# A graph attention layer on one core: wider VectorE instructions in the attention block, and the carried product ahead of the weighted ones

## The chip, the cores and the metric

The kernel runs on one core of one Trainium2 chip. The metric is the device time of one execution in microseconds (us), as the median of several runs. On-chip memory has 128 partitions; a shape like 128x1024 means 128 partitions by 1024 elements of each.

## The reference

The program computes four graph layers, one after the other, on 6250 nodes with 16 features and 206250 edges sorted by their target node: a graph convolution, an edge-conditioned convolution, a sheaf layer and an attention layer. Each is applied to a normalised copy of the features and its result added to them. The change touches the last, the attention layer:

```python
w_m = (efeat @ W_msg + b_msg).reshape(E, in_f, -1)
w_a = (efeat @ W_attn + b_attn).reshape(E, in_f, -1)
h_src = feat[src][:, :, None]
e1 = w_m * h_src
e2 = w_a * h_src
seg_max = jax.ops.segment_max(e2, dst, num_segments=N)
ex = jnp.exp(e2 - seg_max[dst])
denom = jax.ops.segment_sum(ex, dst, num_segments=N)
attn = ex / denom[dst]
ft = jax.ops.segment_sum(e1 * attn, dst, num_segments=N)
return ft.sum(axis=1)
```

`e1` and `e2` have 16 x 16 = 256 elements for each edge.

## The kernel before

**Tiling.** The edges lie in quads: four edges with the same target. Each of the 128 partitions has 440 quads, and the stage "attn" (L2435 to L2815) takes them in 110 blocks of `QB` = 4. For a block, `T` holds two planes (`t` = 0: attention value `e2`; `t` = 1: message `e1`) of 4 quads x 4 edges x 256 elements; `X` holds `exp` of the first plane and its product with the second. `T` has two buffers, chosen by the block's parity, and `X` has one. `walk` (with `At`, which turns a block's number into semaphore values) writes the first and last blocks out and runs the others in a loop of two blocks a turn.

**The engines, each with its own hand-written order:**

- GpSimd (L2513) gathers the source nodes' features (`got`) and the edge lines, 16 + 2 indirect transfers a block. SyncE loads lines and stores the maxima (`tops`) and sums (`sums`) of each block.
- TensorE (L2549): `matrices(at, q)` (L2569) computes for the four edges of quad `q` both 256-element rows into `pw`, in PSUM, once `times` has freed it. `quad_sum(at, q)` adds up the four edges of a quad by four matmuls with the identity (L2578), which wait on `s_prod`, and adds the running sum of the quads before by a fifth (L2585): for quad 0 that is `carried`, for the others the sum that ScalarE has just copied. The order in a block is: `quad_sum` of quads 1, 2, 3 of the block before, each followed by `matrices` of the next block's same quad; then three of four matmuls of `quad_sum(at, 0)`, `matrices(at+2, 0)` in between, and the rest of `quad_sum(at, 0)`.
- ScalarE (L2608): `weights` (L2639) is the exponential of one quad, once all subtractions of the block are done; `scales` computes the factor for the running sum; `put_state` (L2658) copies a quad's running sum from PSUM, which the next `quad_sum` waits for; `tops_out` (L2644) copies the maxima.
- VectorE (L2696), function `a_block`. In order, where `times(nxt, q)` (L2715) multiplies the next block's matrices by the gathered features, two instructions a quad: first half of `times(nxt, 0)`; `larger` over pairs of edges into `two` (L2730), one instruction for two quads; second half of `times(nxt, 0)`; `larger` over what is left (L2730); `forward(0)` (L2737), the running maximum; first half of `times(nxt, 1)`; `forward(1)`; second half; `forward(2)`, `forward(3)`; three `back` (L2743), which carry the maximum back to the first quad, with the subtractions `below` (L2748) of quads 3, 2 and 1 in between; `drop` (L2791) and `below(0)`; `times(nxt, 2)`; `product(0)` (L2755); the running sum times its factor into `carried` (L2799, which waits on ScalarE's factor and last state copy); `product(1)`; `times(nxt, 3)`; `product(2)`, `product(3)`.

`ch.do` counts an instruction on a semaphore of VectorE's own, and `ch.wait(n)` waits until instruction `n` has written its result. `turn_wait` is a wait on a semaphore followed by an increment of another.

## Time and profile before

| what | value |
|---|---|
| time, median of 3 runs | 8973.12 us (8966.02 to 8974.08) |
| span of the profiled execution | 8951.1 us (its own time is not given; the median lies 22.0 us above this span) |
| instructions | 135582 |
| busy share of the span | VectorE 84%, TensorE 81%, GpSimd 71%, ScalarE 54% |
| attention blocks | from about 5805 to 8845 us of the span |

The profile comes from one execution. The engines are called PE (TensorE; PEld is its weight load), DVE (VectorE), ACT (ScalarE), POOL (GpSimd) and SP (SyncE) in it.
### The profile page before, as it was taken

To read this page: it belongs to the slowest core of one execution; us is meant where nothing else is said; L and a number is where in the kernel's file an instruction comes from. 1 tells how busy PE (TensorE), PEld (TensorE's weight loads), DVE (VectorE), ACT (ScalarE), POOL (GpSimd) and SP (SyncE) were. 2 spreads that over 40 slices of the span, in tenths; PEclk is the share of its full clock that TensorE was granted. 3 is DMA by queue.
4 is the path that set the end of the run, shared out by engine and by line. 5 is a ranking of instruction groups with operands and counts; after the bars stand their busy time and mean duration, and the time that the engine had idled before them with its cause. 6 is when DMAs were issued, how large, how long until landed. Compare 5 with 4: busy or idle time off the path is not lost. (4 is left out here: it accounts for less than half of the span.)

```text
span 8951.1 us, 135582 instructions
## 1 busy us (share of the span) xinstructions
PE 7229.0 (81%) x35152; PEld 4078.3 (46%) x35152; DVE 7510.0 (84%) x11807; ACT 4799.3 (54%) x7730; POOL 6388.3 (71%) x6335
## 2 busy tenths in 40 slices
PE   3888857888888088888888889488888888888884
PEld 3776744555555055555555555233333333333331
DVE  7999956777777388888888888499999999999997
ACT  5999956666666056556666656233333333333333
POOL 6777767777776577777777777376777777677674
PEclk9899967888887589999999999789999999999997
DMA  4222221121111111111111111122222222222223
GB/s 154 65 64 61 64 40 44 45 45 46 46 45 38 20 28 28 33 28 33 28 31 29 29 32 17 20 65 82 75 75 76 75 82 76 75 76 75 81 77 99
DMA packets 499695, 493.19 MB, mean 55 GB/s; under 512 B 181075, under 2 KB 396906, under 8 KB 498731
## 3 DMA queue, kind: packets, MB, share of 16 engines
q1 hardware_dynamic: 299595, 371.60, 12.5%
q0 software_dynamic: 199904, 119.78, 9.7%
q14 instruction: 171, 1.40, 0.1%
q8 instruction: 25, 0.41, 0.0%
HBM read 240.96 MB, written 249.95 MB: 55 GB/s over the span
## 5 line engine op out<-in xcount | busy, mean ns | idle before, releaser
L2525 POOL DMA_INDIRECT attn_got<-tab,attn_line x1760 | 1925.6, 1094 | 778.7 <-issue 504.4
L1983 POOL DMA_INDIRECT sheaf_got<-tab,sheaf_idx x1612 | 1692.1, 1050 | 489.9 <-issue 474.8
L2578 PE MATMUL attn_q<-attn_X,ident 128*128 128x512 f32 x3520 | 1716.2, 626 | 101.1 <-ACT attn_S L2658 92.5
L2072 PE MATMUL sheaf_acc<-sheaf_hot_hi,sheaf_wide 128*128 128x392 bf16 x6696 | 1350.5, 344 | 282.7 <-DVE sheaf_hot_hi L2275 280.9
L1508 POOL DMA_INDIRECT nnconv_got<-tab,nnconv_idx x1116 | 1081.9, 969 | 400.0 <-issue 320.9
L2578 PEld LDWEIGHTS attn_q<-attn_X,ident 128*128 128x128 f32 x3520 | 651.4, 198 | 1190.6 <-issue 1190.6
L2715 DVE TENSOR_TENSOR attn_T<-attn_w,attn_got 128x1024 f32<-128x1024 f32 x880 | 1054.5, 1220 | 150.4 <-PE attn_w L2569 115.2
L2658 ACT COPY attn_S<-attn_q 128x512 f32<-128x512 f32 x440 | 255.9, 582 | 1530.4 <-PE attn_q L2585 1530.4
L1173 POOL DMA_INDIRECT gcn_got<-tab,gcn_idx x868 | 825.9, 952 | 302.3 <-issue 274.7
L2072 PEld LDWEIGHTS sheaf_acc<-sheaf_hot_hi,sheaf_wide 128*128 128x128 bf16 x6696 | 653.6, 106 | 819.1 <-issue 489.7
L1267 PE MATMUL gcn_acc<-gcn_hot,pieces 128*128 128x512 f32 x2604 | 740.2, 442 | 193.9 <-ACT gcn_hot L1321 126.6
L2569 PE MATMUL attn_w<-src_hi 32*128 32x512 f32 x3520 | 567.1, 715 | 274.7 <-DVE attn_T L2715 273.7
L1197 DVE SCALAR_TENSOR_TENSOR gcn_hot<-gcn_key,key_of,gcn_one 128x512 fp32r<-128x512 f16 x1116 | 750.4, 743 | 4.2 <-DMA gcn_blk<-src_blk 4.2
L1740 DVE TENSOR_TENSOR nnconv_prod<-nnconv_w,nnconv_got 128x1024 f32<-128x1024 f32 x434 | 490.6, 1143 | 268.0 <-PE nnconv_w L1543 267.4
L1267 PEld LDWEIGHTS gcn_acc<-gcn_hot,pieces 128*128 128x128 f32 x2604 | 541.1, 214 | 323.7 <-issue 202.3
L2134 ACT ACTIVATE sheaf_zT<-sheaf_z,sheaf_b 128x832 f32<-128x832 f32 x248 | 223.2, 951 | 721.6 <-PE sheaf_z L2024 721.6
L2072 PE MATMUL sheaf_acc<-sheaf_hot_act,sheaf_wide 128*128 128x392 bf16 x2976 | 607.4, 343 | 0.0
L1543 PE MATMUL nnconv_w<-nnconv_W,nnconv_tT 64*128 64x256 f32 x3224 | 536.5, 461 | 3.5 <-DVE nnconv_prod L1740 3.5
L1558 PE MATMUL nnconv_acc<-nnconv_hot,pieces 128*128 128x512 f32 x1736 | 527.8, 464 | 11.7 <-ACT nnconv_hot L1639 11.7
L2748 DVE SCALAR_TENSOR_TENSOR attn_T<-attn_T,attn_tops 128x1024 f32<-128x1024 f32 x440 | 533.2, 1212 | 0.0
L2755 DVE SCALAR_TENSOR_TENSOR attn_X<-attn_T,attn_X 128x1024 f32<-128x1024 f32 x440 | 527.2, 1220 | 1.3 <-ACT attn_X L2639 1.3
L2275 DVE TENSOR_SCALAR sheaf_hot_hi<-sheaf_number,src_hi 128x784 bf16<-128x784 f16 x1116 | 478.2, 429 | 51.3 <-PE sheaf_acc L2072 32.8
(508 smaller groups left out, 13738.5 us busy)
## 6 DMA issues: line engine op xcount, KB each, us to landing
sums<-attn_S SPq DMA_DIRECT2D x110, 1024.0 KB, 5.2
tops<-attn_S SPq DMA_DIRECT2D x110, 512.0 KB, 3.0
attn_got<-tab,attn_line POOLq DMA_INDIRECT x1760, 2.4
sheaf_got<-tab,sheaf_idx POOLq DMA_INDIRECT x1612, 2.4
gcn_key<-src_key SPq DMA_DIRECT2D x62, 384.0 KB
gcn_blk<-src_blk SPq DMA_DIRECT2D x62, 384.0 KB
nnconv_got<-tab,nnconv_idx POOLq DMA_INDIRECT x1116
nnconv_key<-src_key SPq DMA_DIRECT2D x62, 256.0 KB
```

Source lines behind the costliest of these rows:

```text
L1173: e.indirect_dma_start(out=got[at.b][:, j, :], out_offset=None, in_=tab[0], in_offset=indices(idx[at.b], j)).then_inc(s_got[at.b], 16)
L1197: hit = e.scalar_tensor_tensor(out=hot[q][:, n, :].rearrange("p (j m) -> p j m", j=GW), in0=key[at.b][:, g, :].rearrange("p (j m) -> p j m ...
L1267: mm = e.matmul(pacc[q][:, :], pieces[:, part, n * NBLK:(n + 1) * NBLK, :].rearrange("p b f -> p (b f)"), hot[q][:, n, :], start=n + part ...
L1508: e.indirect_dma_start(out=got[at.b][:, j, :], out_offset=None, in_=tab[1], in_offset=indices(idx[at.b], j)).then_inc(s_got_of[part][at.b] ...
L1543: mm = [e.matmul(to[:, t * 512 + (j - 2 * g) * 256:t * 512 + (j - 2 * g + 1) * 256], tT[at.b][t * H1:(t + 1) * H1, j * P:(j + 1) * P], W2[ ...
L1983: e.indirect_dma_start(out=got[at.b][:, j, D:D + T2], out_offset=None, in_=tab[2], in_offset=indices(idx[at.b], j)).then_inc(s_got[half][a ...
L2072: mm = e.matmul(pacc[k][:, 0:HH], wide[at.b][half][:, part, col, :], hot[:, k * HH:(k + 1) * HH], start=False, stop=False, skip_group_chec ...
L2525: e.indirect_dma_start(out=got[at.b][:, 4 * q + n, :], out_offset=None, in_=tab[3], in_offset=indices(ids[:, q, n, :], D + 2)).then_inc(s_ ...
L2569: e.matmul(pw[n // 2][:, n % 2 * 512:(n % 2 + 1) * 512], efT[at.b][n * RW:(n + 1) * RW, q, :], Wc[n * RW:(n + 1) * RW, :], start=True, sto ...
L2578: e.matmul(to, ident[:, :], X[:, q, :, n, :], start=n == 0, stop=False)
L2715: e.tensor_tensor(T[at.b][:, q, :, 2 * half:2 * half + 2, :].rearrange("p t n (i o) -> p n t i o", o=D), pw[half].rearrange("p (n t i o) - ...
L2748: e.scalar_tensor_tensor(out=Tb[:, q, 0, :, :], in0=Tb[:, q, 0, :, :], scalar=1.0, in1=ptop[:, q, None, :].to_broadcast([P, 4, CH]), op0=A ...
```

## The change

- `larger` over pairs of edges takes all four quads in one instruction (L2730, 128x2048) instead of two of two quads.
- `below` and `product` take half a block, two quads, in one instruction of 128x2048, and count `s_sub` and `s_prod` twice a block instead of four times. `below` is a plain subtraction now.
- The order is `back(2)`, `back(1)`, `below(1)`, `back(0)`, `drop`, `below(0)`, with a wait after each `back`; quads 2 and 3 are subtracted by `below(1)`, quads 0 and 1 by `below(0)`.
- The product into `carried` comes before `product(0)`, which is now quads 0 and 1; `product(1)`, quads 2 and 3, comes after `times(nxt, 3)`.
- `quad_sum(at, q)` waits for the product of its half; what waits on `s_sub` and `s_prod` elsewhere has the new counts.

```diff
--- before.py
+++ after.py
@@ -2572,7 +2572,7 @@
                     def quad_sum(at, q, between=None):
 
                         to = pq.rearrange("p (t c) -> p t c", t=2)
-                        turn_wait(e, s_prod, at.of(QB, q + 1))
+                        turn_wait(e, s_prod, at.of(2, q // 2 + 1))
                         turn_wait(e, s_state, at.of(QB, q + 2))
                         for n in range(4):
                             e.matmul(to, ident[:, :], X[:, q, :, n, :], start=n == 0, stop=False)
@@ -2633,14 +2633,14 @@
 
                     def weights(at, q):
 
-                        e.wait_ge(s_sub, at.of(QB, QB))
+                        e.wait_ge(s_sub, at.of(2, 2))
                         if at.k > 0:
                             e.wait_ge(s_quad, at.of(QB, q + 1 - QB))
                         e.activation(X[:, q, 0, :, :], T[at.b][:, q, 0, :, :], ACT.Exp).then_inc(s_x, 1)
 
                     def tops_out(at):
 
-                        e.wait_ge(s_sub, at.of(QB, QB))
+                        e.wait_ge(s_sub, at.of(2, 2))
                         e.copy(S[at.b][:, :, 0:CH], ptop).then_inc(s_copied, 1)
 
                     def scales(at):
@@ -2706,7 +2706,7 @@
                     def times(at, q, halves=(0, 1)):
 
                         if q == 0 and at.k >= 2 and 0 in halves:
-                            e.wait_ge(s_prod, at.of(QB, -QB))
+                            e.wait_ge(s_prod, at.of(2, -2))
                         if q % 2 == 0 and 0 in halves:
                             e.wait_ge(s_got[q // 2][at.b], at.half(16 * EH, 16 * EH))
                         for half in halves:
@@ -2744,24 +2744,25 @@
                                 out=ptop[:, q, :], in0=ptop[:, q + 1, :], scalar=apart_q[:, bass.ds(at.of(QB, q + 1), 1)],
                                 in1=Sb[:, q, 0:CH], op0=ALU.add, op1=ALU.max))
 
-                        def below(q):
-                            e.scalar_tensor_tensor(
-                                out=Tb[:, q, 0, :, :], in0=Tb[:, q, 0, :, :], scalar=1.0,
-                                in1=ptop[:, q, None, :].to_broadcast([P, 4, CH]), op0=ALU.mult, op1=ALU.subtract).then_inc(s_sub, 1)
-
-                        def product(q):
-
-                            e.wait_ge(s_x, at.of(QB, q + 1))
+                        def below(half):
+                            q = slice(half * QB // 2, (half + 1) * QB // 2)
+                            e.tensor_tensor(Tb[:, q, 0, :, :], Tb[:, q, 0, :, :],
+                                            ptop[:, q, None, :].to_broadcast([P, QB // 2, 4, CH]),
+                                            ALU.subtract).then_inc(s_sub, 1)
+
+                        def product(half):
+
+                            q = slice(half * QB // 2, (half + 1) * QB // 2)
+                            e.wait_ge(s_x, at.of(QB, (half + 1) * QB // 2))
                             e.scalar_tensor_tensor(out=X[:, q, 1, :, :], in0=Tb[:, q, 1, :, :], scalar=1.0,
                                                    in1=X[:, q, 0, :, :], op0=ALU.mult, op1=ALU.mult).then_inc(s_prod, 1)
 
                         if more:
                             times(nxt, 0, (0,))
                         e.wait_ge(s_t, at.of(2 * QB, 2 * QB + 2))
-                        for q in range(0, QB, 2):
-                            n = ch.do(larger(two[:, q:q + 2, :, :].rearrange("p q n c -> p q (n c)"),
-                                             Tb[:, q:q + 2, 0, 0:2, :].rearrange("p q n c -> p q (n c)"),
-                                             Tb[:, q:q + 2, 0, 2:4, :].rearrange("p q n c -> p q (n c)")))
+                        n = ch.do(larger(two[:, :, :, :].rearrange("p q n c -> p q (n c)"),
+                                         Tb[:, :, 0, 0:2, :].rearrange("p q n c -> p q (n c)"),
+                                         Tb[:, :, 0, 2:4, :].rearrange("p q n c -> p q (n c)")))
                         if more:
                             times(nxt, 0, (1,))
                         if at.k >= 2:
@@ -2784,33 +2785,33 @@
                             ch.wait(n)
                             n = forward(q)
                         ch.wait(n)
-                        for q in range(QB - 2, -1, -1):
-                            n = back(q)
-                            below(q + 1)
-                            ch.wait(n)
+                        n = back(2)
+                        ch.wait(n)
+                        n = back(1)
+                        below(1)
+                        ch.wait(n)
+                        ch.wait(back(0))
                         e.scalar_tensor_tensor(out=drop[:, :], in0=So[:, QB - 1, 0:CH], scalar=1.0, in1=ptop[:, 0, :],
                                                op0=ALU.mult, op1=ALU.subtract).then_inc(s_top, 1)
                         below(0)
                         if more:
                             times(nxt, 2)
-                        product(0)
                         e.wait_ge(s_scale, at.of(1, 1))
                         e.wait_ge(s_state, at.of(QB, 2))
                         e.scalar_tensor_tensor(out=carried[:, :].rearrange("p (t c) -> p t c", t=2),
                                                in0=So[:, QB - 1, CH:].rearrange("p (t c) -> p t c", t=2), scalar=1.0,
                                                in1=scale[:, None, :].to_broadcast([P, 2, CH]),
                                                op0=ALU.mult, op1=ALU.mult).then_inc(s_carried, 1)
-                        product(1)
+                        product(0)
                         if more:
                             times(nxt, 3)
-                        product(2)
-                        product(3)
+                        product(1)
 
                     for k in range(2):
                         ids_of(At(k))
                     for q in range(QB):
                         times(At(0), q)
-                    walk(e, NBQ, a_block, ch, 3 + QB + QB - 1, head=4)
+                    walk(e, NBQ, a_block, ch, 2 + QB + QB - 1, head=4)
                     e.wait_ge(s_state, NBQ * QB + 2)
             banks.close()
```

VectorE in the loop, from the first `back` to the last subtraction, before the change (`attn_tops` is the maximum, L2743 `back`, L2748 `below`, L2791 `drop`):

```order
L2743 SCALAR_TENSOR_TENSOR attn_tops<-attn_tops,apart_q,attn_S 128x256
L2748 SCALAR_TENSOR_TENSOR attn_T<-attn_T,attn_tops 128x1024
L2743 SCALAR_TENSOR_TENSOR attn_tops<-attn_tops,apart_q,attn_S 128x256
L2748 SCALAR_TENSOR_TENSOR attn_T<-attn_T,attn_tops 128x1024
L2743 SCALAR_TENSOR_TENSOR attn_tops<-attn_tops,apart_q,attn_S 128x256
L2748 SCALAR_TENSOR_TENSOR attn_T<-attn_T,attn_tops 128x1024
L2791 SCALAR_TENSOR_TENSOR src_lo<-attn_S,attn_tops 128x256
L2748 SCALAR_TENSOR_TENSOR attn_T<-attn_T,attn_tops 128x1024
```

The same place with the change (L2749 `below`, L2794 `drop`):

```order
L2743 SCALAR_TENSOR_TENSOR attn_tops<-attn_tops,apart_q,attn_S 128x256 x2
L2749 TENSOR_TENSOR attn_T<-attn_T,attn_tops 128x2x1024
L2743 SCALAR_TENSOR_TENSOR attn_tops<-attn_tops,apart_q,attn_S 128x256
L2794 SCALAR_TENSOR_TENSOR src_lo<-attn_S,attn_tops 128x256
L2749 TENSOR_TENSOR attn_T<-attn_T,attn_tops 128x2x1024
```

Two `back` now stand side by side, and the four subtractions have become two, the first of them behind the second `back`.

VectorE right behind that place, from `times(nxt, 2)` to the last product, before the change (L2715 `times`, L2755 `product`, L2799 `carried`):

```order
L2715 TENSOR_TENSOR attn_T<-attn_w,attn_got 128x2x2x256 x2
L2755 SCALAR_TENSOR_TENSOR attn_X<-attn_T,attn_X 128x1024
L2799 SCALAR_TENSOR_TENSOR src_lo<-attn_S,src_lo 128x512
L2755 SCALAR_TENSOR_TENSOR attn_X<-attn_T,attn_X 128x1024
L2715 TENSOR_TENSOR attn_T<-attn_w,attn_got 128x2x2x256 x2
L2755 SCALAR_TENSOR_TENSOR attn_X<-attn_T,attn_X 128x1024 x2
```

The same place with the change (L2757 `product`, L2801 `carried`):

```order
L2715 TENSOR_TENSOR attn_T<-attn_w,attn_got 128x2x2x256 x2
L2801 SCALAR_TENSOR_TENSOR src_lo<-attn_S,src_lo 128x512
L2757 SCALAR_TENSOR_TENSOR attn_X<-attn_T,attn_X 128x2x1024
L2715 TENSOR_TENSOR attn_T<-attn_w,attn_got 128x2x2x256 x2
L2757 SCALAR_TENSOR_TENSOR attn_X<-attn_T,attn_X 128x2x1024
```

`carried` has moved ahead of the first product, and each product has twice the size.

The orders of `matrices` and `quad_sum` on TensorE and of all work on ScalarE, GpSimd and SyncE are as before.

## Rows read from the trace of the kernel before

**Rows 1.** Windows: length, busy us of PE, PEld, DVE, ACT, POOL, clock, DMA, GB/s

```profile
6000.00:8800.00 2800.00, 2471.09 (x7788) 950.92 (x7787) 2642.12 (x2975) 1001.26 (x1845) 1971.10 (x1828) 0.96 0.26 76
```

**Rows 2.** Waits of the attention stage: who for whom, us in total, times, longest

```profile
DVE attn_T L2715 <- PE attn_w L2569: 110.6, 110, 1.9
```

**Rows 3.** Tile src_lo: count, ns min/median/max, first and last start, forms

```profile
L2791 DVE SCALAR_TENSOR_TENSOR src_lo<-attn_S,attn_tops x110: 410/416/421, 5840.3 to 8812.9; 128x256 f32<-128x256 f32 x110
```

**Rows 4.** Timeline of VectorE: start us, us, instruction, [idle before, releaser]

```profile
7008.43 1.23 DVE L2715 TENSOR_TENSOR attn_T<-attn_w,attn_got 128x1024 f32<-128x1024 f32 x1 [1.21 <-PE attn_w L2569]
...
7011.10 0.48 DVE L2737 SCALAR_TENSOR_TENSOR attn_S<-attn_S,apart_q 128x256 f32<-128x256 f32 x1
7011.71 0.49 DVE L2737 SCALAR_TENSOR_TENSOR attn_tops<-attn_S,apart_q 128x256 f32<-128x256 f32 x1
7012.24 0.49 DVE L2743 SCALAR_TENSOR_TENSOR attn_tops<-attn_tops,apart_q,attn_S 128x256 f32<-128x256 f32 x1
...
7013.77 0.49 DVE L2743 SCALAR_TENSOR_TENSOR attn_tops<-attn_tops,apart_q,attn_S 128x256 f32<-128x256 f32 x1
7014.16 1.21 DVE L2748 SCALAR_TENSOR_TENSOR attn_T<-attn_T,attn_tops 128x1024 f32<-128x1024 f32 x1
...
7018.27 2.35 DVE L2715 TENSOR_TENSOR attn_T<-attn_w,attn_got 128x1024 f32<-128x1024 f32 x2
7020.54 1.22 DVE L2755 SCALAR_TENSOR_TENSOR attn_X<-attn_T,attn_X 128x1024 f32<-128x1024 f32 x1
7021.67 0.69 DVE L2799 SCALAR_TENSOR_TENSOR src_lo<-attn_S,src_lo 128x512 f32<-128x512 f32 x1
7022.27 1.22 DVE L2755 SCALAR_TENSOR_TENSOR attn_X<-attn_T,attn_X 128x1024 f32<-128x1024 f32 x1
7023.41 2.35 DVE L2715 TENSOR_TENSOR attn_T<-attn_w,attn_got 128x1024 f32<-128x1024 f32 x2
...
7035.46 1.23 DVE L2715 TENSOR_TENSOR attn_T<-attn_w,attn_got 128x1024 f32<-128x1024 f32 x1 [0.66 <-PE attn_w L2569]
...
7050.44 2.35 DVE L2715 TENSOR_TENSOR attn_T<-attn_w,attn_got 128x1024 f32<-128x1024 f32 x2
...
7062.94 1.23 DVE L2715 TENSOR_TENSOR attn_T<-attn_w,attn_got 128x1024 f32<-128x1024 f32 x1 [1.15 <-PE attn_w L2569]
```

**Rows 5.** Timeline of TensorE, then of ScalarE, over the same block

```profile
7020.77 1.14 PE L2569 MATMUL attn_w<-src_hi 32*128 32x512 f32 x8 [1.98 <-DVE attn_T L2715]
7022.15 2.81 PE L2578 MATMUL attn_q<-attn_X,ident 128*128 128x512 f32 x6 [0.24 <-issue]
7025.91 1.14 PE L2569 MATMUL attn_w<-src_hi 32*128 32x512 f32 x8 [0.95 <-DVE attn_T L2715]
...
7034.19 1.14 PE L2569 MATMUL attn_w<-src_hi 32*128 32x512 f32 x8
...
7019.36 0.57 ACT L2658 COPY attn_S<-attn_q 128x512 f32<-128x512 f32 x1
7019.82 2.95 ACT L2639 ACTIVATE attn_X<-attn_T 128x1024 f32<-128x1024 f32 x3
...
7029.00 0.59 ACT L2658 COPY attn_S<-attn_q 128x512 f32<-128x512 f32 x1 [4.15 <-PE attn_q L2585]
```

**Rows 6.** Groups of VectorE behind the loop: 2048 elements; busy, mean ns, idle

```profile
L2964 DVE TENSOR_TENSOR attn_times<-attn_st,attn_inv 128x2048 f32<-128x2048 f32 x5 | 11.5, 2293 | 13.5 <-ACT attn_inv L2898 13.5
```

**Rows 7.** Windows in a block with a lower granted clock, and right behind it

```profile
7048.00:7051.50 3.50, 3.50 (x11) 0.99 (x10) 3.50 (x4) 3.50 (x6) 3.04 (x2) 0.51 0.07 9
7051.75:7055.00 3.25, 3.25 (x14) 1.08 (x13) 3.25 (x3) 0.21 (x1) 2.69 (x2) 1.00 0.82 245
```

**Rows 8.** Timeline of TensorE in that block

```profile
7047.81 1.86 PE L2569 MATMUL attn_w<-src_hi 32*128 32x512 f32 x8 [1.99 <-DVE attn_T L2715]
7049.60 3.77 PE L2578 MATMUL attn_q<-attn_X,ident 128*128 128x512 f32 x6
7053.30 1.14 PE L2569 MATMUL attn_w<-src_hi 32*128 32x512 f32 x8
```

## The prediction

> **What bounds the kernel now.** I read the shares of the span first, then the waits of the attention stage, then one block of it in order of time on VectorE and TensorE, and last the granted clock. The change touches only this stage. Over 2800 us of it VectorE is busy for 2642 us (94%), TensorE for 2471 us (88%) and GpSimd for 1971 us [rows 1]; by that alone VectorE would be the bound. The waits say otherwise: VectorE waits 110 times, once per block, for `attn_w`, 110.6 us in all, for TensorE's matrices [rows 2]. So the block runs round a circle through both engines. A block is 27.27 us long on average (first and last start of L2791, 109 steps) [rows 3].
>
> I follow the circle from the first half of `times(nxt, 1)`, which VectorE starts at 7008.43, to the same one at 7035.46: 27.03 us [rows 4].
> - VectorE: 3.81 us to the first `back` at 7012.24, 6.03 us of `back`, `below` and `drop` to `times(nxt, 2)` at 7018.27, 2.27 us to `product(0)` at 7020.54, then `carried`, `product(1)` and `times(nxt, 3)`, which ends at 7025.76: 17.33 us in all [rows 4].
> - TensorE: 0.15 us later it computes `matrices(at+2, 0)` at 7025.91, the last two matmuls of `quad_sum(at, 0)`, ScalarE copies them at 7029.00, `quad_sum(at, 1)` follows and then `matrices(.., 1)` at 7034.19, and VectorE goes on at 7035.46: 9.55 us [rows 5].
>
> In these 9.7 us VectorE does its last products, the pairwise maximum and the rest, and then stands idle for 0.66 to 1.21 us [rows 4]. What is saved there is saved in the idle time. What is late between `times(nxt, 1)` and `matrices(at+2, 0)` lengthens every block.
>
> One thing on this circle has slack, and the change spends it: the first three products of `quad_sum(at, 0)`. TensorE starts them at 7022.15, 0.39 us after `product(0)` ended at 7021.76, and they take 2.81 us, done at 7024.96 [rows 4, 5]. TensorE then idles 0.95 us for `times(nxt, 3)` [rows 5].
>
> **The change part by part.** Steps from start to start on VectorE are 0.60 us for 512 elements and 1.13 us for 1024 [rows 4], so 512 elements cost 0.53 us and the fixed part is 0.07 us. A 2048 instruction gives 1.13 + 1.07 = 2.20 us to the next, with an end after 2.29 us, as its nearest row has it [rows 6]. Its bounds are the fixed part gone or doubled, 2.13 and 2.27. That `below` becomes a plain subtraction costs nothing: that row is a TENSOR_TENSOR and fits.
> - Pairwise maximum, two instructions to one: 0.07 us less, off the circle, under VectorE's idle time. Worth 0; without that cover 0.07 us a block.
> - `below`, four to two, one `back` without cover: 2 x 0.07 less. But `back(2)` and `back(0)` are now followed at once by what needs them. A dependent step is 0.53 us (7011.71 to 7012.24), a covered one 0.39 (7013.77 to 7014.16) [rows 4]: 2 x 0.14 more. Bounds: nothing, and 0.22 each (the step from 7011.10 to 7011.71 is 0.61). I take 0.14, the same pair of operations' nearest row. The piece goes from 6.03 to 6.03 - 0.14 + 0.28 = 6.17 us.
> - `carried` ahead of the products: it starts 2.27 us after `times(nxt, 2)`. ScalarE's last state copy, which it waits for, ends 1.66 us after (7019.36 + 0.57) [rows 4, 5]: 0.6 us to spare, no wait. Nobody needs it sooner.
> - Products, four to two. The first starts 2.87 us after `times(nxt, 2)`; the exponential of quad 1 ends about 2.6 us after (the second of three from 7019.82 in 2.95 us) [rows 5]: 0.27 us to spare. It saves 0.07 on the circle. The second saves 0.07 off it.
> - **What is handed to TensorE.** `quad_sum` now waits for two quads. The first product ended 3.49 us after the start of `times(nxt, 2)`; now the signal comes after 2.27 + 0.60 + 2.29 = 5.16 us, 1.67 us later. Queued behind this wait on TensorE are `quad_sum(at, 0)`, then `matrices(at+2, 0)` and all that follows. The SP queue (state stores) and GpSimd's gathers are paced by copies and spare time: GpSimd is busy 70% of the stage [rows 1], so I cost them at nothing.
>
> The new circle: VectorE 3.81 + 6.17 + 5.16 = 15.14 us to the end of the first product. TensorE 0.39 us, then six half-products (three matmuls) 2.74 us (2.81 less the 0.07 by which the next overlaps in rows 8, from 7049.60 to 7053.30), after which `matrices(at+2, 0)` can start, 3.13 us after the product's end, while `times(nxt, 3)` was done at 2.27 and would have allowed 2.42. Then the old 9.55. Sum 15.14 + 3.13 + 9.55 = 27.82 us against 27.03, so 0.79 more. The bound of the signal's delay is 0.15 (7025.76 to 7025.91) to 0.39; with the other bounds the circle lies between 27.4 and 28.1. VectorE alone comes to 27.03 - 0.66 - 0.35 + 0.28 = 26.3 us, so it isn't the bound.
>
> **The clock.** In other blocks TensorE's granted clock is lower: 0.51 of 2.4 GHz from 7048.0 to 7051.5, so 1.2 GHz, and 1.00 from 7051.75 [rows 7]. It had idled 1.99 us for `times(nxt, 2)` before [rows 8]. In the stretch the matrices took 1.86 us for 1.14 and the six matmuls 3.77 for 2.81; `matrices(at+2, 0)` started 0.51 us after `times(nxt, 3)` ended, for 0.15 [rows 4, 5, 8]. That block is 27.48 us (7035.46 to 7062.94) [rows 4], only 0.45 more: the slack took the rest. The mean of 27.27 says that about half of the blocks or more are such. In the changed kernel TensorE idles 2.1 us, computes matrices for 1.14, and idles again for 1.9 (from 3.64 to 5.55 us after `times(nxt, 2)`), and then comes the work that has no slack. I expect the fall in nearly every block. If it comes with the matrices, as in rows 8, the stretch of 3.5 us ends 0.45 us after the work began and costs 0.2; if it comes at the work's start or later, it costs half of 3.5, 1.75. The middle is 1.0; I take 1.15, since the second idle piece lies right ahead of the work and makes a late fall likelier.
> The Trainium skill (TensorE: Matmul & The Clock Gate, Terms) prices a throttled stretch at its length times one less K/N, so half. By that each fall would have cost 1.75 us already before, where the trace shows 0.45; it would give the upper case below.
>
> Sum: 27.82 + 1.15 = 28.97 us a block against 27.27, 1.70 more; for 108 blocks 184 us. 8951 + 184 = 9135 as span; the median of the runs is 22 us above the span of the profiled one, so **9157 us**.
>
> **The rivals.**
> - A. The clock costs no more than it does now. Then only the circle grows: 27.82 - 27.27 = 0.55 us a block, 60 us, 9033. For it: in the block of rows 4 the same idle of 1.98 us [rows 5] brought no fall. Against it: the idle doubles. 10%.
> - B. Each fall costs its half in full: 27.82 + 1.75 - 27.27 = 2.30, 248 us, 9221. For it: all that follows the late signal is without slack. 12%.
> - C. Not slower: VectorE sets the block. This holds if TensorE takes up the delay in `quad_sum(at, 0)`, for which its three matmuls would have to be through 2.4 us after the product's end; at 0.39 + 2.74 us they miss by 0.7. The busy shares in rows 1 speak for it, the 110 waits in rows 2 against it. Five instructions fewer at 0.07 are 0.35 a block; with the two exposed waits 0.07 is left, 8 us (8965); with the waits covered 38 us (8935). 7%.
> The Trainium skill (Perfetto Trace Analysis, Optimizing Scalar/DVE Operations) says that larger operations help a saturated VectorE, with about 60 ns of overhead for an instruction on SBUF and 125 ns with PSUM; by that, as an estimate, C would save 3 x 0.06 + 2 x 0.125 = 0.43 us a block, 46 us (8927). The same section says that where VectorE is not saturated but makes others idle, breaking instructions up may finish work sooner, which speaks against this change; the waits in rows 2 put this kernel there.
> - That the change doesn't do what it says can be left out: the order shows the merged instructions in the loop.
>
> **How the numbers follow.** My forecast, with clock costs between 0.6 and 1.5 us, has 71% and spans about 9095 to 9200. With A's and B's neighbourhoods and the bounds of the circle the range is 9070 to 9230, which leaves out A itself and C. About 18 us (0.2%) is what a measurement of this kernel tells from no change. Faster by more: 4% (C with covered waits). Within: 3% (C). Slower: 93%.
>
> **What would show it.** In the changed profile the 128x2048 products should take about 2.29 us; the first `quad_sum(at, 0)` matmul should start 0.4 us after the first product ends; `matrices(at+2, 0)` should come over 0.8 us after `times(nxt, 3)` ends; VectorE's wait for `attn_w` should grow from 1.0 to about 2.6 us a block; and the mean clock of the stage should fall below 0.96. Blocks of 27.8 with a clock of 0.96 would be A. If VectorE waits no longer than before and the block is 27.2 or less, my circle is wrong. If it waits for `attn_X` of ScalarE or for the state copy ahead of `carried`, I mis-sized the spare time there.

## The result and the profile after

| | before | changed |
|---|---|---|
| time, median | 8970.73 us (4 runs) | 9338.22 us (4 runs) |
| ratio of the times, 95% interval | 1 | 1.0416 (1.0402 to 1.0431) |
| span of the profiled execution | 8951.1 us | 9340.3 us |

The changed kernel is 4.2% slower, 367 us. 9157 us and a range of 9070 to 9230 had been forecast: the direction was right, the size was not. Executions that lie more than 1.5% above the fastest one of the same kernel are left out of the ratios; this touches only `carried_first_only`, further down.

From the page of the changed kernel, the busy times of the engines and the groups of the quad sums (L2578) and of `times` (L2715), with mean ns of one and idle time before:

```profile
PE 7436.1 (80%) x35152; PEld 4161.8 (45%) x35152; DVE 7488.2 (80%) x11257; ACT 4798.6 (51%) x7730; POOL 6558.7 (70%) x6335
...
L2578 PE MATMUL attn_q<-attn_X,ident 128*128 128x512 f32 x3520 | 1940.5, 696 | 302.2 <-DVE attn_X L2757 210.4
...
L2715 DVE TENSOR_TENSOR attn_T<-attn_w,attn_got 128x1024 f32<-128x1024 f32 x880 | 1053.2, 1217 | 520.7 <-PE attn_w L2569 509.9
```

The stage's windows, as [rows 1]:

```profile
6000.00:8800.00 2800.00, 2359.19 (x6936) 907.60 (x6934) 2335.39 (x2192) 887.47 (x1640) 1906.81 (x1647) 0.89 0.22 68
```

VectorE was busy for 2335 us in this stretch, 307 us less than before, and TensorE for 112 us less, although its matmuls have become longer. Fewer blocks pass in the same time, and all engines wait more. The waits, as [rows 2]:

```profile
DVE attn_T L2715 <- PE attn_w L2569: 507.6, 216, 2.9
...
PE attn_q L2578 <- DVE attn_X L2757: 210.4, 110, 4.2
```

VectorE's wait for `attn_w` grew from 110.6 to 507.6 us. The second row is new: TensorE waits once per block for the wide product. The length of a block, as [rows 3]:

```profile
L2794 DVE SCALAR_TENSOR_TENSOR src_lo<-attn_S,attn_tops x110: 420/421/423, 5855.8 to 9191.7; 128x256 f32<-128x256 f32 x110
```

(9191.7 - 5855.8) / 109 = 30.60 us, for 27.27: 3.33 x 109 = 363 us, nearly all of the 367.

VectorE in one block, as [rows 4]:

```profile
7012.58 1.22 DVE L2715 TENSOR_TENSOR attn_T<-attn_w,attn_got 128x1024 f32<-128x1024 f32 x1 [1.83 <-PE attn_w L2569]
...
7016.39 1.02 DVE L2743 SCALAR_TENSOR_TENSOR attn_tops<-attn_tops,apart_q,attn_S 128x256 f32<-128x256 f32 x2
...
7022.57 2.35 DVE L2715 TENSOR_TENSOR attn_T<-attn_w,attn_got 128x1024 f32<-128x1024 f32 x2
7024.84 0.68 DVE L2801 SCALAR_TENSOR_TENSOR src_lo<-attn_S,src_lo 128x512 f32<-128x512 f32 x1
7025.44 2.28 DVE L2757 SCALAR_TENSOR_TENSOR attn_X<-attn_T,attn_X 128x2048 f32<-128x2048 f32 x1
7027.64 2.35 DVE L2715 TENSOR_TENSOR attn_T<-attn_w,attn_got 128x1024 f32<-128x1024 f32 x2
...
7043.36 1.23 DVE L2715 TENSOR_TENSOR attn_T<-attn_w,attn_got 128x1024 f32<-128x1024 f32 x1 [2.04 <-PE attn_w L2569]
```

TensorE in it, as [rows 5, 8]:

```profile
7025.07 1.14 PE L2569 MATMUL attn_w<-src_hi 32*128 32x512 f32 x8 [2.13 <-DVE attn_T L2715]
7028.11 5.46 PE L2578 MATMUL attn_q<-attn_X,ident 128*128 128x512 f32 x6 [1.90 <-DVE attn_X L2757]
7033.50 1.36 PE L2569 MATMUL attn_w<-src_hi 32*128 32x512 f32 x8
```

The block goes from 7012.58 to 7043.36, 30.78 us. `back` starts after 3.81 us, `times(nxt, 2)` 6.18 later, the first product ends 5.15 after that (7027.72), and the quad sum starts 0.39 later: each as forecast. Then it takes 5.46 us for 2.81. From the start of `matrices(at+2, 0)` at 7033.50 the rest of the block takes 9.86 us for 9.55, 0.22 of it in the matrices themselves (1.36 for 1.14). The reason stands in the windows, as [rows 7]: TensorE busy is the first number with a bracket, the clock is the third from the end.

```profile
7003.50:7027.00 23.50, 19.81 (x70) 7.59 (x62) 20.43 (x21) 7.54 (x13) 18.32 (x18) 1.00 0.09 18
7027.25:7034.00 6.75, 5.89 (x10) 2.35 (x14) 4.93 (x4) 1.97 (x5) 2.04 (x2) 0.50 0.70 240
7034.00:7057.50 23.50, 20.00 (x70) 7.61 (x65) 20.16 (x21) 7.31 (x13) 18.32 (x18) 1.00 0.09 20
```

From 7027.25 to 7034.0, that is 6.75 us, the granted clock is 0.50: 1.2 GHz instead of 2.4. It begins about 1.0 us into TensorE's second idle piece (7026.21 to 7028.11), and of its 6.75 us TensorE works 5.89. Before, such a stretch lasted 3.5 us, and it came in about six of ten blocks: a mean clock of 0.96 over 2800 us [rows 1] makes (1 - 0.96) x 2 x 2800 / 3.5 = 64 stretches in 103 blocks.

### The profile page after: what moved, and what is told of

Its sections match the earlier page's. It is cut to its first block and busy times, and to the rows that moved or that the text cites. A ratio compares the mean times of both kernels' runs of the same rounds, so it can differ in the third digit from the quotient of the medians.

```text
span 9340.3 us, 135296 instructions
## 1 busy us (share of the span) xinstructions
PE 7436.1 (80%) x35152; PEld 4161.8 (45%) x35152; DVE 7488.2 (80%) x11257; ACT 4798.6 (51%) x7730; POOL 6558.7 (70%) x6335
## 5 line engine op out<-in xcount | busy, mean ns | idle before, releaser
L2525 POOL DMA_INDIRECT attn_got<-tab,attn_line x1760 | 2069.8, 1176 | 976.4 <-issue 503.5
L2578 PE MATMUL attn_q<-attn_X,ident 128*128 128x512 f32 x3520 | 1940.5, 696 | 302.2 <-DVE attn_X L2757 210.4
L1983 POOL DMA_INDIRECT sheaf_got<-tab,sheaf_idx x1612 | 1713.9, 1063 | 490.0 <-issue 474.9
L2715 DVE TENSOR_TENSOR attn_T<-attn_w,attn_got 128x1024 f32<-128x1024 f32 x880 | 1053.2, 1217 | 520.7 <-PE attn_w L2569 509.9
L2578 PEld LDWEIGHTS attn_q<-attn_X,ident 128*128 128x128 f32 x3520 | 710.8, 215 | 1431.4 <-issue 1431.4
L2569 PE MATMUL attn_w<-src_hi 32*128 32x512 f32 x3520 | 530.1, 672 | 256.8 <-DVE attn_T L2715 255.8
L2639 ACT ACTIVATE attn_X<-attn_T 128x1024 f32<-128x1024 f32 x440 | 440.4, 1051 | 148.0 <-DVE attn_T L2749 147.9
L2757 DVE SCALAR_TENSOR_TENSOR attn_X<-attn_T,attn_X 128x2048 f32<-128x2048 f32 x220 | 501.7, 2281 | 0.2 <-ACT attn_X L2639 0.2
```

The lines of the kernel that those rows point to most:

```text
L1983: e.indirect_dma_start(out=got[at.b][:, j, D:D + T2], out_offset=None, in_=tab[2], in_offset=indices(idx[at.b], j)).then_inc(s_got[half][a ...
L2525: e.indirect_dma_start(out=got[at.b][:, 4 * q + n, :], out_offset=None, in_=tab[3], in_offset=indices(ids[:, q, n, :], D + 2)).then_inc(s_ ...
L2569: e.matmul(pw[n // 2][:, n % 2 * 512:(n % 2 + 1) * 512], efT[at.b][n * RW:(n + 1) * RW, q, :], Wc[n * RW:(n + 1) * RW, :], start=True, sto ...
L2578: e.matmul(to, ident[:, :], X[:, q, :, n, :], start=n == 0, stop=False)
L2715: e.tensor_tensor(T[at.b][:, q, :, 2 * half:2 * half + 2, :].rearrange("p t n (i o) -> p n t i o", o=D), pw[half].rearrange("p (n t i o) - ...
```

## The experiments

Two theories stood after this. **Signal and clock:** TensorE gets its signal 1.67 us later, which costs 0.55 us a block on the circle, and because it has idled before it, the clock is low while the first quad sum runs, now for twice as long, which costs nearly 3 us. **Width:** the wide instructions themselves cost the time, on VectorE or by holding up another engine. `signal` is how long after the start of `times(nxt, 2)` the first product's signal comes; the kernel before has 3.49 us. "Ratio" is to the kernel before on the same chip.

### The signal without the wide instructions, and the clock held up

late_signal:

```diff
-                        turn_wait(e, s_prod, at.of(QB, q + 1))
+                        turn_wait(e, s_prod, at.of(2, q // 2 + 1))
...
-                            e.wait_ge(s_prod, at.of(QB, -QB))
+                            e.wait_ge(s_prod, at.of(2, -2))
...
+                            if q % 2 == 1:
+                                done.then_inc(s_prod, 1)
...
-                        product(0)
                         e.wait_ge(s_scale, at.of(1, 1))
                         e.wait_ge(s_state, at.of(QB, 2))
...
+                        product(0)
                         product(1)
```

> The kernel before with every instruction as narrow as it was, carried moved ahead of the products, and the signal to TensorE given only once after each pair of products. The signal comes 2.27 + 0.60 + 1.13 + 1.22 = 5.22 us after the start of the second times, as in the changed kernel (5.15). Signal theory: what costs is when TensorE gets its signal, not how wide the instructions are; block 30.7 us with the long low clock, time 9320 to 9350. Rival, the wide instructions cost through GpSimd, whose gathers stand up to 2.9 us for 0.94 beside a wide VectorE instruction with two operands in on-chip memory: then this kernel loses little and stays under 9100.

late_signal_warm adds two groups of two extra matmuls a block to it, called `warm`, the first behind `quad_sum(at-1, 3)` and ahead of `matrices(at+1, 3)`, the second ahead of `quad_sum(at, 0)`. Nobody reads their result:

```diff
+                    def warm(at, count):
+
+                        turn_wait(e, s_ef, at.of(1, 2))
+                        for n in range(count):
+                            e.matmul(pturn[:, :], ident[:, :], Wc[:, :], start=True, stop=True)
...
                                 quad_sum(prev, q)
+                            if q == 3 and 2 and at.k < NBQ - 2:
+                                warm(at.plus(2), 2)
...
+                        if 2 and at.k < NBQ - 2:
+                            warm(at.plus(2), 2)
```

> late_signal with the four extra matmuls of after_warm in TensorE's two idle pieces. In after_warm the quad sum took 2.75 us at clock 1.00, as expected, but the block was 29.2 us for 27.8, and VectorE waited for attn_got, with gathers of 2.9 us beside the wide products. If the wide instructions make GpSimd the bound there, the narrow ones here leave it free: block 27.8 us, 9030 us, clock 1.00, no wait for attn_got. If the extra matmuls themselves slow the gathers, it stays near 9160 as after_warm did.

late_signal took 9331.4 us, ratio 1.0407 (1.0391 to 1.0423): with no wide instruction in it, it loses as much as the whole change. Its quad sum, behind the idle time, in TensorE's timeline:

```profile
7022.99 1.14 PE L2569 MATMUL attn_w<-src_hi 32*128 32x512 f32 x8 [1.99 <-DVE attn_T L2715]
7026.10 5.46 PE L2578 MATMUL attn_q<-attn_X,ident 128*128 128x512 f32 x6 [1.98 <-DVE attn_X L2755]
```

And the stage's window:

```profile
6000.00:8700.00 2700.00, 2280.36 (x6682) 875.19 (x6680) 2264.84 (x2549) 857.10 (x1584) 1691.12 (x1582) 0.89 0.23 68
```

late_signal_warm took 9031.5 us, ratio 1.0074 (1.0059 to 1.0090). The stage's window, and the tile row that gives the length of a block:

```profile
6000.00:8700.00 2700.00, 2587.37 (x8159) 1009.63 (x8152) 2502.67 (x2816) 947.57 (x1749) 1909.23 (x1749) 1.00 0.25 75
```

```profile
L2803 DVE SCALAR_TENSOR_TENSOR src_lo<-attn_S,attn_tops x110: 417/420/422, 5854.7 to 8882.1; 128x256 f32<-128x256 f32 x110
```

The clock is 1.00 and a block (8882.1 - 5854.7) / 109 = 27.77 us, where the sum had 27.82. The circle with this run's own terms (6.03 us for the narrow subtractions, 5.22 for the signal) gives 27.74. The two runs part the loss: 300 us, 2.8 a block, are the clock's, and 65 us are left above the kernel before, which has low stretches of its own. The width theory falls for the changed kernel as it stands.

### The changed kernel with the clock held up

after_warm is the changed kernel with the same `warm` groups, by the same lines.

> The changed kernel with two extra 128x512 matmuls in each of TensorE's two idle pieces of a block (behind the last quad sum of the block before, and behind the matrices of quad 3); their result goes to the PSUM bank of the turned lines, after it has been copied, and is read by nobody. Clock theory: of the 3.3 us that a block got longer, 0.55 is the circle through the late signal and about 2.9 (against 0.1 before) the low granted clock while the first quad sum runs. With the idle filled the clock stays at 1.00, the six entries of that quad sum take 2.8 us for 5.46, a block takes 27.8 us (30.6 in the changed kernel), and the time is 8971 + 0.55 x 108 = 9030 us. Rival, the wide instructions or the late signal alone cost it all and the low clock only accompanies the waiting: time stays at 9338 or rises by the extra work. If the clock is the cause but two matmuls are too few, the clock lies between 0.89 and 1.00 and the time between.

It took 9159.5 us, ratio 1.0218 (1.0201 to 1.0235): 179 of the expected 308 us came back. The quad sum did what the clock theory said (TensorE's timeline; L2591 is the extra work):

```profile
7011.40 1.14 PE L2569 MATMUL attn_w<-src_hi 32*128 32x512 f32 x8 [0.66 <-DVE attn_T L2725]
7012.47 1.98 PE L2591 MATMUL attn_turn<-src_hi,ident 128*128 128x512 f32 x4
7014.44 2.81 PE L2578 MATMUL attn_q<-attn_X,ident 128*128 128x512 f32 x6
7017.19 1.14 PE L2569 MATMUL attn_w<-src_hi 32*128 32x512 f32 x8
```

Six entries take 2.81 us. But VectorE has a new wait:

```profile
DVE attn_T L2725 <- DMA attn_got<-tab,attn_line: 209.4, 74, 3.4
```

`attn_got` is what GpSimd gathers. The wait is not there from the start. Between 6000 and 6900 us of the span, tile `src_lo` and VectorE's waits (L2725 is `times`) are

```profile
L2804 DVE SCALAR_TENSOR_TENSOR src_lo<-attn_S,attn_tops x33: 420/421/422, 6000.4 to 6893.7; 128x256 f32<-128x256 f32 x33
DVE attn_T L2725 <- PE attn_w L2569: 50.5, 32, 1.7
DVE attn_T L2725 <- DMA attn_got<-tab,attn_line: 3.0, 8, 0.5
```

and between 7100 and 8700 us

```profile
L2804 DVE SCALAR_TENSOR_TENSOR src_lo<-attn_S,attn_tops x55: 420/421/422, 7122.9 to 8697.0; 128x256 f32<-128x256 f32 x55
DVE attn_T L2725 <- DMA attn_got<-tab,attn_line: 179.4, 55, 3.4
```

So the first blocks take 893.3 / 32 = 27.92 us, with VectorE waiting for TensorE as in the sum of 27.82, and the later ones 1574.1 / 54 = 29.15 us, with VectorE waiting once per block for the gathers. (The expectation of late_signal_warm speaks of 29.2 us; the mean over the whole stage is 28.63.) VectorE and GpSimd in the later pattern (L2759 is `below`, L2767 `product`):

```profile
7006.71 2.28 DVE L2759 TENSOR_TENSOR attn_T<-attn_T,attn_tops 128x2048 f32<-128x2048 f32 x1
...
7011.77 2.28 DVE L2767 SCALAR_TENSOR_TENSOR attn_X<-attn_T,attn_X 128x2048 f32<-128x2048 f32 x1
...
7016.24 2.28 DVE L2767 SCALAR_TENSOR_TENSOR attn_X<-attn_T,attn_X 128x2048 f32<-128x2048 f32 x1
```

```profile
7006.99 0.96 POOL L2525 DMA_INDIRECT attn_got<-tab,attn_line  x1 [0.30 <-DMA attn_got<-tab,attn_line]
7008.25 0.94 POOL L2525 DMA_INDIRECT attn_got<-tab,attn_line  x1 [0.30 <-issue]
...
7012.00 2.87 POOL L2525 DMA_INDIRECT attn_got<-tab,attn_line  x1 [0.30 <-issue]
...
7016.43 2.90 POOL L2525 DMA_INDIRECT attn_got<-tab,attn_line  x1 [0.31 <-issue]
```

An undisturbed gather takes 0.94 us. The one that starts at 7012.00 takes 2.87 and the one at 7016.43 takes 2.90: each ended soon after the wide product it had met. Beside `below`, which is just as wide but takes one operand from PSUM, they stay at 0.96 and 0.94. The same holds from 6500 to 7100 us: the 87 gathers that met only a `below` took 0.94 to 0.96 us, the 59 that met only a wide product 1.06 to 2.96. A narrow product does it too, but less: in the kernel before, gathers beside one took 0.94 to 1.44 us. The group of gathers from 6000 to 8700 us, before and in after_warm:

```profile
L2525 POOL DMA_INDIRECT attn_got<-tab,attn_line x1581 | 1733.6, 1097 | 720.3 <-issue 452.6 <-DMA attn_line<-quad_lines 267.7
L2525 POOL DMA_INDIRECT attn_got<-tab,attn_line x1506 | 1938.3, 1287 | 459.0 <-issue 430.3 <-DMA attn_got<-tab,attn_line 28.0 <-DMA attn_line<-quad_lines 0.6
```

The mean is 1287 ns for 1097 before, and the waits for lines (267.7 us before) are gone. Gathers, line gathers and the idle time before them (1938.3 + 246.2 + 459.0 + 57.3 us in 2700) fill the stretch. That alone does not make GpSimd the bound: it was as full between 6000 and 6900 us (900.9 us in 900), where VectorE hardly waited for it. So there is a second cost, and the width theory holds for it: in the later blocks the wide instructions make the gathers come too late, and VectorE waits. Against late_signal_warm, which has the same extra work and narrow instructions, it is 128 us. Why the pattern tips at about 7000 us is not shown. In the changed kernel itself, with blocks of 30.6 us, VectorE waited only 4 times for gathers, 10.7 us in all.

### The change one part at a time

products_only has the products merged to two; `carried` stays behind the first, and all else is as before.

> The kernel before with only the products merged to two (two quads each), carried where it was, behind the first. The signal comes 2.27 + 2.29 = 4.56 us after the start of the second times. Signal theory: circle 3.81 + 6.03 + 4.56 + 3.13 + 9.55 = 27.1 us at full clock, TensorE's second idle piece 1.3 us; with a clock that stays low as long as in the changed kernel (half of 5 us and more in the quad sum) 29 to 30.2 us. So 9100 to 9290, most of the loss, between first_split and the changed kernel. Rival, the subtractions and the pairwise maximum are to blame: within 0.3% of the kernel before, 8971.

```diff
                         product(0)
                         e.wait_ge(s_scale, at.of(1, 1))
...
-                        product(1)
                         if more:
                             times(nxt, 3)
-                        product(2)
-                        product(3)
+                        product(1)
```

with `product` and the counts of `s_prod` as in the change. 9247.3 us, ratio 1.0311 (1.0293 to 1.0328), clock 0.90 in the stage: most of the loss. The signal did not come at the expected 4.56 us, though, but later:

```profile
7024.28 2.34 DVE L2715 TENSOR_TENSOR attn_T<-attn_w,attn_got 128x1024 f32<-128x1024 f32 x2
7026.91 2.29 DVE L2756 SCALAR_TENSOR_TENSOR attn_X<-attn_T,attn_X 128x2048 f32<-128x2048 f32 x1 [0.29 <-ACT attn_X L2639]
```

7026.91 + 2.29 - 7024.28 = 4.92 us. Without `carried` ahead of it, the wide product waits for ScalarE's second exponential, here for 0.29 us and 32.7 us over the stage.

subtract_only has `below` and the counts of `s_sub` as in the change:

```diff
-                        for q in range(QB - 2, -1, -1):
-                            n = back(q)
-                            below(q + 1)
-                            ch.wait(n)
+                        n = back(2)
+                        ch.wait(n)
+                        n = back(1)
+                        below(1)
+                        ch.wait(n)
+                        ch.wait(back(0))
```

> The kernel before with only the subtractions merged to two, with the new order of the back instructions. By the sum 0.14 us a block more on the circle (two exposed waits less two fixed parts), 15 us; the signal comes no later after the second times than before. Signal theory: 8971 to 9000. Rival, the wide subtraction with its two exposed waits makes TensorE idle longer and brings the long low clock: over 9060.

8965.7 us, ratio 1.0000 (0.9991 to 1.0010): no difference.

pairs_only has the pairwise maximum as in the change:

```diff
-                        for q in range(0, QB, 2):
-                            n = ch.do(larger(two[:, q:q + 2, :, :].rearrange("p q n c -> p q (n c)"),
...
+                        n = ch.do(larger(two[:, :, :, :].rearrange("p q n c -> p q (n c)"),
```

> The kernel before with only the pairwise maximum as one instruction. It is off the circle, so the 0.07 us a block go into VectorE's wait for attn_w: 8967, same. If VectorE's own work set the block, 8 us less; if the wide instruction slows GpSimd enough to count, more.

8958.6 us, ratio 0.9995 (0.9985 to 1.0005): no difference.

These two results say less than they seem to. By the tile rows of `drop`, a block takes 27.27 us in the kernel before, in subtract_only and in pairs_only, with mean clocks in the stage of 0.96, 0.98 and 0.96. While the clock falls now and then, a small change of the circle can be taken up by more or fewer low stretches; times_first, further down, is a case of it. So the runs show that neither part brings the loss, and not what each would cost at a steady clock.

carried_first_only moves the carried product ahead of `product(0)`, and nothing else:

```diff
-                        product(0)
                         e.wait_ge(s_scale, at.of(1, 1))
                         e.wait_ge(s_state, at.of(QB, 2))
...
+                        product(0)
                         product(1)
```

> The kernel before with only carried moved ahead of the first product. The signal comes 4.09 us after the second times, as in first_split, which took 8972. Signal theory: the same here, 8965 to 8985; the slack of the first quad sum takes most of the 0.6 us. Rival, the move itself makes VectorE wait for ScalarE's last state copy: a wait of src_lo for attn_S once per block.

Ratio 1.0033 (1.0017 to 1.0049). Its seven runs scatter: 8985, 8988, 8993, 9011, 9147, 9158 and one of 13433 us. The ratio takes the lowest four, whose median is 8990 us; the median of all seven is 9010.8. The profile at hand is of the one of 9147, so nothing on the time is read from it; in it VectorE did not wait for the state copy, so the expected wait of the rival is absent. 8990 us is just above what I wrote down.

### Half of it undone

first_split:

```diff
-                        turn_wait(e, s_prod, at.of(2, q // 2 + 1))
+                        turn_wait(e, s_prod, at.of(3, min(q, 2) + 1))
...
-                        product(0)
+                        product(0, 1)
+                        product(1, 2)
...
-                        product(1)
+                        product(2, 4)
```

> The changed kernel with the first of its two products split in two instructions again, each with its own signal; carried stays ahead of them, the second product stays wide. The signal for the first quad sum then comes 2.27 + 0.60 + 1.22 = 4.09 us after the start of the second times, instead of 5.16 (3.49 before). Signal theory: the first quad sum starts 1.07 us sooner; on the circle 15.14 - 1.07 + 3.13 + 9.55 = 26.8 us or, since times(nxt, 3) then ends 0.1 later than the quad sum, 27.1 us at full clock, and TensorE's second idle piece is 0.84 us for 1.90. Without a fall that is 8973 us or less; with the low clock in most blocks, which now has only little slack, up to 28.9, 9150. I expect 9030 to 9150, so at least half of the 367 us gone. Rival, the wide subtraction and the wide maximum cost the time: it stays above 9250.

8972.5 us, ratio 1.0011 (1.0001 to 1.0020). All but 9 us of the loss is gone, more than expected. TensorE in one block:

```profile
7033.20 1.14 PE L2569 MATMUL attn_w<-src_hi 32*128 32x512 f32 x8 [2.22 <-DVE attn_T L2715]
7035.18 2.81 PE L2578 MATMUL attn_q<-attn_X,ident 128*128 128x512 f32 x6 [0.84 <-DVE attn_X L2757]
7038.33 1.14 PE L2569 MATMUL attn_w<-src_hi 32*128 32x512 f32 x8 [0.34 <-DVE attn_T L2715]
```

It idles 0.84 us ahead of the quad sum for 1.90, and the mean clock of the stage is 0.99. GpSimd in the stage, and VectorE's waits:

```profile
L2525 POOL DMA_INDIRECT attn_got<-tab,attn_line x1583 | 1788.5, 1130 | 482.7 <-issue 453.1 <-DMA attn_got<-tab,attn_line 29.6
L2536 POOL DMA_INDIRECT attn_line<-in_lines,attn_line_at x198 | 370.3, 1870 | 60.4 <-issue 60.4
...
DVE attn_T L2715 <- PE attn_w L2569: 103.9, 108, 2.1
...
DVE attn_T L2715 <- DMA attn_got<-tab,attn_line: 6.7, 2, 4.4
```

Busy and idle time together are 2702 us of 2700, so GpSimd never waits for lines. But VectorE waits for `attn_w` as in the kernel before, and only twice for gathers: that GpSimd sets the block of 27.3 us here is not shown. Nor is it settled why the clock fell so seldom in this kernel: carried_first_only has the same signal, and its mean clock over the whole execution was 0.886 to 0.888 in the four runs that count, for 0.897 to 0.901 here.

### Can the circle be made shorter?

before_warm is the kernel before with the first `warm` group alone:

```diff
                                 quad_sum(prev, q)
+                            if q == 3 and 2 and at.k < NBQ - 2:
+                                warm(at.plus(2), 2)
```

> The kernel before with two extra matmuls in TensorE's one idle piece (behind quad sum 3). The clock stays at 1.00 in all blocks, each takes the 27.03 us of an undisturbed block for 27.27 on average: 26 us less, 8940. Rival, the extra matmuls cost something (they delay the matrices of quad 3 or slow the gathers): same or slower.

8937.5 us, ratio 0.9969 (0.9958 to 0.9979): a block of 27.03 us at clock 1.00, as expected. 29 us is what the low clock cost the kernel before. Against before_warm, late_signal_warm is 94 us slower, with the clock up in both: that is the late signal, together with whatever its second `warm` group costs.

times_first:

```diff
                         product(0)
+                        if more:
+                            times(nxt, 3)
                         e.wait_ge(s_scale, at.of(1, 1))
...
                         product(1)
-                        if more:
-                            times(nxt, 3)
```

> The kernel before with times(nxt, 3) right behind the first product, ahead of carried and the second product; all instructions as before. TensorE's first quad sum was waiting for nothing but this in its middle: circle 3.81 + 6.03 + 3.49 + 3.13 + 9.55 = 26.0 us, VectorE's own work 26.4. At full clock 26.5 us a block, 8890. But the slack that hid the low clock is gone, and with it up to 1.75 us more in blocks where the clock falls: 27.3 to 27.8. I expect 8900 to 9010, most likely within 0.5% of the kernel before. If the circle theory is wrong (VectorE alone sets the block), nothing changes and VectorE's wait for attn_w stays near 1 us.

8965.8 us, ratio 0.9999 (0.9990 to 1.0008): no difference, inside the expectation. VectorE waited 101.2 us for `attn_w`, close to 1 us a block, so by itself this run looks as if the circle theory were wrong; the next one decides it. The window of the stage:

```profile
6000.00:8700.00 2700.00, 2408.87 (x7516) 925.29 (x7514) 2554.33 (x2870) 960.90 (x1779) 1871.49 (x1783) 0.95 0.26 77
```

times_first_warm adds the first `warm` group to it:

> times_first with the two extra matmuls of before_warm. If the low clock ate what the new order gained, the block now falls to the larger of the circle (26.0 us) and VectorE's own work (26.4 plus a wait of up to 0.3 for the matrices of quad 3): 26.4 to 26.7 us, so 60 to 95 us under the kernel before, 8870 to 8905. If times_first was stopped by something else (GpSimd at 24.8 us a block, state copies), it stays near before_warm, 8937.

8886.4 us, ratio 0.9910 (0.9893 to 0.9926). The window, and VectorE's wait for `attn_w`:

```profile
6000.00:8700.00 2700.00, 2521.82 (x8130) 992.54 (x8131) 2616.42 (x2950) 986.88 (x1824) 1981.88 (x1835) 1.00 0.27 79
```

```profile
DVE attn_T L2725 <- PE attn_w L2569: 31.2, 110, 1.3
```

The wait fell from 110.6 to 31.2 us, and VectorE is busy for 97% of the stretch: now it is nearly the bound. Neither edit gives this alone: the order gained nothing while the clock fell, and the clock alone gained 29 us of the 76. This version beats both kernels.

> times_first_warm with the pairwise maximum as one instruction. VectorE is the bound there by my sum, so 0.07 us a block count at last: 7 us under times_first_warm. Against it: the wide instruction holds up a gather of GpSimd by up to 2 us, but at 24.8 us a block it has 1.6 to spare. Within 0.1% of times_first_warm either way.

It has the edit of pairs_only on top. 8883.3 us, ratio 0.9905 (0.9889 to 0.9922), so 3 us from times_first_warm, inside its scatter.

## Why the prediction was wrong

- **What bounds the kernel:** right. The circle through both engines was confirmed term by term, and late_signal_warm, with the late signal and the clock up, gave 27.77 us for the 27.82 of the sum (27.74 with its own terms). The first blocks of after_warm, with the wide instructions, took 27.92.
- **Pairwise maximum worth nothing:** right (pairs_only). **Subtractions, 0.14 us a block more:** the piece took 6.18 us for 6.17. The 15 us do not show in the time of subtract_only, where the low stretches can have taken them up.
- **`carried` ahead without a wait:** right for VectorE. That the move alone delays the signal by 0.6 us, and what this costs by itself (28 us in carried_first_only), I had not weighed.
- **The late signal:** right, 5.15 us for 5.16.
- **The clock: the term that failed.** That it would fall in every block was right. The step that failed is "the stretch of 3.5 us ... costs half of 3.5, 1.75": I took the length of the low stretch from the kernel before [rows 7] as fixed. It was 6.75 us in the changed kernel, beginning in the second idle piece, 0.9 us ahead of the work, and nearly all of the work up to `matrices(at+2, 0)` fell into it. The quad sum took 2.65 us more and the rest of the block behind it 0.3 more, about 3.0 a block in place of the 1.15 taken and of the 1.75 that was the upper end. late_signal, against late_signal_warm, gives 2.8. That the second idle piece is what kept the clock down for longer is my reading; no run tests it by itself. Put into the sum, 27.8 + 3.0 gives 30.8 for the measured 30.78. The range, which hung on the same 3.5, was too low for the same reason.
- **GpSimd costed at nothing:** right for the changed kernel, and by luck. Its gathers became longer (1176 ns for 1097), which the sum did not have, and only the long blocks left room for it: after_warm shows VectorE waiting for gathers in blocks of 29.15 us. It also shows blocks of 27.92 with the same instructions, so whether rival A's 9033 us was within reach stays open.
- **The Trainium skill's price** (TensorE: Matmul & The Clock Gate, Terms) of half the throttled length comes near the changed kernel: it gives 3.4 us for a stretch of 6.75, and about 3.0 were lost, since TensorE worked only 5.89 us of it. What the page Perfetto Trace Analysis (Optimizing Scalar/DVE Operations) in the Trainium skill says, that breaking up instructions may let work finish sooner where VectorE makes other engines idle, agrees with first_split: 8972 us for 9338.

## What to carry to other kernels

Where two engines hand work to and fro, the time of the first signal can count for far more than the number of instructions: merging two instructions delays what the first half would have released by the whole second half. In this kernel a second wait of 1.9 us on TensorE cost about 3 us more behind it, since the clock was low when the work came. If such a wait can't be removed, it is worth trying to fill it: extra matmuls into a free bank held the clock up here and cost less than the low clock did. A change that shortens the circle may show nothing until the clock is held too, so try both together.

## What the runs showed of the hardware

- The stretch at 1.2 GHz has no fixed length. It was 3.5 us where TensorE had idled 2.0 us and worked nearly without a break afterwards, and 6.75 us where it idled 2.1 us, worked 1.1, idled 1.9 and then worked.
- A GpSimd gather (0.94 us) that meets a VectorE product with both operands in on-chip memory outside PSUM (SBUF) waits for it: 2.87 and 2.90 us beside 2.28 us of product. Beside `below`, of the same length and with an operand in PSUM, it doesn't (0.94 to 0.96). The Trainium skill (SBUF — State Buffer, SBUF: two separate sides) says that VectorE and GpSimd share a port pair that one of them holds for a whole instruction, also when VectorE has two SBUF inputs and the GpSimd operation reads SBUF; these rows agree with it.
- One kernel can run in two patterns within one execution: after_warm's blocks took 27.92 us between 6000 and 6900 us of its span and 29.15 between 7100 and 8700, at a clock of 1.00 in both.
- While the clock falls now and then, kernels with different circles can come out alike: 27.27 us a block in the kernel before (clock 0.96) and 27.28 in times_first (0.95). With the clock held up they were 27.03 (before_warm) and 26.53 (times_first_warm).
